# Flamingo block with routed-expert attention: VectorE's gate inversion moved ahead of round 1's row maxima, GpSimd's next mixture begun ahead of the third pair's sums

## The reference

```python
q = (x @ Wq).reshape(b, t, h, dh).transpose(0, 2, 1, 3)
k = (x @ Wk).reshape(b, t, h, dh).transpose(0, 2, 1, 3)
gl_v = (x @ Ws).reshape(b, t, h, e)
wv = _topk_mask(gl_v, SEL) * jax.nn.sigmoid(gl_v)
xv = jnp.einsum('btd,edk->btek', x, Wv)
v = jnp.einsum('bthe,btek->bhtk', wv, xv)
probs = jax.nn.softmax(jnp.einsum('bhid,bhjd->bhij', q * scale, k), axis=-1)
attn = jnp.einsum('bhij,bhjd->bihd', probs, v)
gl_o = (x @ Wd).reshape(b, t, h, e)
out = jnp.einsum('bthe,bthk,ekd->btd', _topk_mask(gl_o, SEL), attn, Wo)
```

## Time and profile before

| | us |
|---|---|
| median of 3 runs | 1139.66 (1139.25 to 1140.4) |
| the profiled execution's own time | 1140.54 |
| its span in the profile | 1138.8 |
| TensorE busy | 1103.0 (97%) |
| VectorE busy | 926.2 (81%) |
| GpSimd busy | 657.9 (58%) |
| ScalarE busy | 568.1 (50%) |

### The profile page before, as it was taken

The page is one execution under the profiler, slowest core; times in us unless marked ns, Lnnn a source line. Parts: engine busy times, 40 slices in busy tenths (PEclk is TensorE's granted clock), DMA queues, the critical chain, the costliest instruction groups (busy, mean ns, idle before and its releaser), DMA issues.

```text
span 1138.8 us, 18705 instructions
## 1 busy us (share of the span) xinstructions
PE 1103.0 (97%) x5709; PEld 836.8 (73%) x5709; DVE 926.2 (81%) x1609; ACT 568.1 (50%) x1295; POOL 657.9 (58%) x476
## 2 busy tenths in 40 slices
PE   7999999999999999999999999999999999999988
PEld 6888888888888888886676766767667666767655
DVE  7988787878777775768798797887988987988986
ACT  7634444444444443436556555455556555555533
POOL 2645252525243433328849669489398497595793
PEclk9999999999999999999999999999999999999999
DMA  5441414141414122343333524424326235244241
GB/s 204 148 139 47 130 56 129 55 129 55 129 55 129 55 92 93 131 130 83 103 76 110 166 55 147 129 55 150 108 59 199 74 94 161 77 116 121 53 134 38
DMA packets 89277, 119.97 MB, mean 105 GB/s; under 512 B 9120, under 2 KB 52896, under 8 KB 89248
## 3 DMA queue, kind: packets, MB, share of 16 engines
q1 hardware_dynamic: 89248, 119.61, 35.1%
HBM read 58.76 MB, written 16.78 MB: 66 GB/s over the span
## 4 chain that ended last, share of the span: by engine, by line
PE 68%; POOL 13%; DVE 9%; issue 5%; ACT 4%; POOLq 0%; DMA 0%; DVEq 0%; ACTq 0%
PE ps_f L992 23%; PE ps_s L992 8%; PE ps_o L2297 7%; PE ps_h L992 7%; POOL spare L1610 6%; PE ps_r L2219 6%; POOL spare L1616 5%; PE ps_r L2252 5%; PE ps_s L2273 4%; PE ps_r L2228 3%; DVE nmax L1880 2%; DVE beaten L1969 1%; POOL z L1628 1%; ACT tmp L1701 1%; ACT probs_odd L1701 1%
## 5 line engine op out<-in xcount | busy, mean ns | idle before, releaser
L1610 POOL TENSOR_TENSOR spare<-xv,pick 128x512 f32<-128x512 f32 x160 | 185.2, 1157 | 35.2 <-DVE pick L1996 22.3
L1880 DVE TENSOR_REDUCE nmax<-ps_s 128x1 f32<-128x512 f32 x256 | 158.6, 681 | 55.0 <-PE ps_s L2273 54.0
L1628 POOL TENSOR_TENSOR z<-z,z_tmp 128x1280 f32<-128x1280 f32 x35 | 102.7, 2934 | 123.5 <-DVE z_tmp L1900 121.0
L1616 POOL TENSOR_TENSOR spare<-spare 128x512 f32<-128x512 f32 x128 | 165.8, 1295 | 10.0
L1701 ACT ACTIVATE tmp<-ps_s,nmax 128x512 f32<-128x512 f32 x124 | 85.5, 689 | 109.5 <-DVE nmax L1880 109.5
L2297 PE MATMUL ps_o<-pt,spare 128*64 128x512 f32 x496 | 115.7, 609 | 9.2 <-POOL spare L1616 5.1
L254 POOL TENSOR_TENSOR e_t<-e_t 128x512 fp32r<-128x512 f32 x28 | 35.4, 1297 | 135.6 <-ACT e_t L510 135.6
L2273 PE MATMUL ps_s<-k,q 64*128 64x512 f32 x768 | 106.3, 408 | 0.7 <-ACT pt L1710 0.7
L2273 PEld LDWEIGHTS ps_s<-k,q 64*128 64x128 f32 x768 | 67.3, 184 | 47.3 <-issue 34.3
L254 POOL TENSOR_TENSOR c<-stage,c 128x512 fp32r<-128x512 f32 x28 | 41.5, 1514 | 95.8 <-ACT c L250 95.8
L2219 PE MATMUL ps_r<-es_t,c_t 128*128 128x512 f32 x384 | 96.3, 399 | 0.0
(11 more groups left out here) (253 smaller groups left out, 2279.1 us busy)
## 6 DMA issues: line engine op xcount, KB each, us to landing
pt<-tmp SPq DMA_DIRECT2D x248, 128.0 KB, 2.6
stage<-in_x SPq DMA_DIRECT2D x32, 256.0 KB, 3.1
x_sb<-in_x SPq DMA_DIRECT2D x8, 1024.0 KB, 5.3
x_dram<-x_sb SPq DMA_DIRECT2D x32, 256.0 KB, 3.2
stage<-x_dram SPq DMA_DIRECT2D x8, 1024.0 KB, 5.5
x_sb<-x_dram SPq DMA_DIRECT2D x8, 1024.0 KB, 5.6
out_dram<-x_sb SPq DMA_DIRECT2D x31, 256.0 KB, 2.7
pt<-probs_odd SPq DMA_DIRECT2D x60, 128.0 KB, 2.7
```

The lines of the kernel that those rows point to most:

```text
L1610: pool.tensor_tensor(v_tmp[:] if e else acc, xv[:, :, e, :].unsqueeze(2).broadcast_to(shape), pick[:, e, :, 2 * p:2 * p + 2].unsqueeze(3). ...
L1616: pool.tensor_tensor(acc, acc, v_tmp[:], ALU.add).then_inc(v_steps, 1)
L1628: pool.tensor_tensor(zv, zv, z_tmp[:, h % 2], ALU.add).then_inc(z_pool, 1)
L1880: dve.tensor_reduce(nmax[:, n:n + 1], ps_s[:, n % BANKS, :], AX_X, ALU.max, negate=True).then_inc(nmax_ready, 1)
```

## The change

VectorE's `invert` and `route_values` of a batch move from round 1, place SCORES, behind the four row maxima, to round 0, place TURNS, right behind `count_values`. On GpSimd `mix_values` takes a range of experts, and the first mixture of batch b+1 is split: experts 0 and 1 (two products and one sum) ahead of the sums of the third pair (heads 4 and 5) of batch b, experts 2 to 4 behind them. The waits for the pick, the expert values and the earlier values product now stand ahead of the first part.

```diff
+        EARLY = 2
...
-            def mix_values(b, p, first=False):
+            def mix_values(b, p, first=False, experts=range(E)):
...
-                if p == 0:
+                if p == 0 and 0 in experts:
                     pool.wait_ge(pick_ready, b + 1)
                     pool.wait_ge(xv_ready, b * NT + NT)
...
-                if not first:
+                if not first and 0 in experts:
 
                     pool.wait_ge(o_ps, b * PAIRS - PAIRS + p + 1)
...
-                for e in range(E):
+                for e in experts:
...
+            def turn_of(b):
+
+                mix_values(b + 1, 0, experts=range(EARLY))
+                mix_sums(b, LAST_PAIR - 1)
+                mix_values(b + 1, 0, experts=range(EARLY, E))
+
             mix_values(0, 0, True)
             rest(0, True)
             with pool.Fori(0, B - 2) as b:
-                mix_sums(b, LAST_PAIR - 1)
-                mix_values(b + 1, 0)
+                turn_of(b)
                 rest(b + 1)
-            mix_sums(B - 2, LAST_PAIR - 1)
-            for p in range(PAIRS):
+            turn_of(B - 2)
+            for p in range(1, PAIRS):
                 mix_values(B - 1, p)
...
                     if 0 <= n < ROUNDS:
                         for tile in range(n * BANKS, n * BANKS + BANKS):
                             row_max(b, tile)
-                    if n == 1:
-                        invert(b)
-                        route_values(b, first)
...
                         compare(b)
                         count_better(b)
                         count_values(b)
+                        invert(b)
+                        route_values(b, first)
```

## The result

| | median us | range, runs | ratio to before |
|---|---|---|---|
| before | 1140.40 | 1139.25 to 1140.92, 7 | |
| changed | 1144.03 | 1142.65 to 1145.17, 7 | 1.0033 [1.0022, 1.0045] |

The change makes the kernel slower by 3.6 us (2.5 to 5.1). The forecast was 1145.5 us (+5.9) with a range from 1142 to 1150 and 0.90 on slower: side and range hold, and the size is over by 2.3 us. The profiled execution took 1142.79 us, its span is 1141.0.

A forecast was written before the change was run, and what follows sets the result against it. The prediction took TensorE's in-order queue as the bound, so only TensorE's waits lengthen a batch. 7 x (1.49 - 0.73) + 0.54 = +5.9 us gave 1145.5 us, with a range from 1142 to 1150.

The forecast's parts named there:

- Insertion: VectorE's moved block ahead of round 1's q difference and row maxima makes these 1.80 us late.
- Loss in round 1: TensorE waits for late exponentials at tile 7's transposes: 1.80 - 0.31 = 1.49 us in each of 7 loop batches.
- The slack: Round 1, tile 7's transposes: they could start at 740.56 but start near 740.87, so 0.31 us is free.
- GpSimd's wait: TensorE's wait for GpSimd's mixture ahead of the first pair's values product goes: 0.73 us a batch.
- Blocking: GpSimd and VectorE sums holding each other up: no change counted, 0.3 us either way per batch for the range.
- the lower end of my range: Insertion of 1.67 and no z wait left (0.24 a batch): +3.1 us, so 1142.8, rounded out to 1142.
- The first batch: Outside the loop: the whole 1.80 us lost, a 1.26 us wait gone, net +0.54 us.
- The 1.26: First batch: TensorE's wait at 559.47, through ScalarE's logits copy held by GpSimd's mixtures, goes: 1.26 us.
- (a): Rival, faster: transposes have more slack, TensorE does not feel late exponentials, only removed waits count: 1133.3 us; chance 0.06.
- (b): Rival, no difference: VectorE and ScalarE catch up, most of the 1.0 us expert projections wait goes: 1139.3 us; chance 0.04.
- (c): Rival: GpSimd's shifted instructions block VectorE's two sums by a whole instruction each: 1157 us, half gives 1151; chance 0.05.
- (d): Rival: a pause makes the granted clock fall, a values product takes 6.12 us instead of 3.65: 1163 us; chance 0.02.

The follow-up runs named there:

- experiment 1: Kernel before with VectorE's half alone (reciprocal, pick and mask moved; GpSimd's order as before): 1143.64 us, ratio 1.0034.
- the doses: Kernels with insertions of 0, 0.28, 1.13 and 1.80 us, which lost 0.02, 0.11, 0.98 and 1.62 us in the part with round 1.
- experiment 3: Kernel before with GpSimd's half alone, but one early product ahead of the third pair's sums instead of two: 1135.04 us, ratio 0.9956.
- experiment 4: Kernel before with the reciprocal alone moved ahead of the q difference and the maxima: 1141.88 us, ratio 1.0015.
- experiments 6 and 7: First: kernel before, last batch's turned-block moves issued ahead of the residual load, 1139.00 us. Second: that together with experiment 3, 1131.52 us.

## Why the prediction was right, and where its size was off

**Insertion, 1.80 forecast.** 1.80 in the change and in experiment 1.

**Loss in round 1, 1.49 forecast, 1.62 measured.** ScalarE's last read, relative to the batch's start, is 1.83 later (742.49 + 0.21 = 742.70, against 740.51, less the 0.36 by which this batch started later):

```profile
742.49 0.21 ACT L1707 ACTIVATION_READ_ACCUMULATOR spare<-ps_s,nmax 128x1 f32 x1
```

Tile 7's transposes start 0.05 behind it, as forecast. The slack was mis-sized. Half of the eight's 0.96 gave 740.87 for tile 7's start before; TensorE's timeline of before has it at 740.82:

```profile
740.82 0.60 PE L2281 MATMUL ps_s<-ident,spare 128*128 128x128 f32 x4
```

So the slack was 0.26 and not 0.31, and with the read 1.83 late 1.57 is lost at that point. The other 0.05 is a term that I had not seen: tile 7's four transposes take 0.58 to the start of the values product when a wait releases them (742.75 to 743.33), and took 0.53 in the row of eight (740.82 to 741.35). The usable slack is therefore about 0.2, which the doses confirm. The three terms (0.03, 0.05 and 0.05) add 7 x 0.13 = 0.9 us to the sum.

**GpSimd's wait, -0.73.** It is gone, but I gave the credit to the wrong edit. My own numbers could have told: the old mixture would have ended near 762.0 (761.89 + 0.13), and TensorE arrives at 762.65 in any case. Experiment 1 shows it gone with GpSimd untouched. The sum is the same either way; the verdict on the two halves isn't.

**Blocking, "I count no change".** This is the step that failed most. The second part of the batch is 1.07 shorter, and the 0.73 is not all of it. TensorE's timeline of before, to be laid beside the rows from 759.90 on above:

```profile
757.95 0.60 PE L2281 MATMUL ps_s<-ident,spare 128*128 128x128 f32 x4
758.72 0.66 PE L2281 MATMUL ps_s<-ident,spare 128*128 128x128 f32 x4 [0.18 <-ACT spare L1701]
759.62 1.53 PE L2242 MATMUL ps_r<-ident,z 128*128 128x128 f32 x12 [0.25 <-DVE z L1911]
```

From the z transposes to the values product it was 2.27 (759.62 to 761.89) and is 1.46, as in experiments 1 and 3: the mixture's wait was worth 0.81, 0.08 more than its listed 0.73. Up to the z transposes it was 18.27 from the fourth pair's product (741.35 to 759.62) and is 18.01 (743.33 to 761.34): the other **0.26**. Most of it lies between round 3's transposes and those of z, 1.67 before (757.95 to 759.62) and 1.44 now. The eight alone take 0.96, so the waits in this place have shrunk and not gone. They hang on VectorE's two sums of z: the first stands ahead of round 3's row maxima, the second ahead of the z transposes. These took 1.72 and 2.07 in that batch before. In the changed kernel:

```profile
753.71 1.62 DVE L1917 TENSOR_TENSOR z<-z,z_tmp 128x1280 f32<-128x1280 f32 x1
...
759.38 1.90 DVE L1917 TENSOR_TENSOR z<-z,z_tmp 128x1280 f32<-128x1280 f32 x1
```

GpSimd's instructions beside them:

```profile
752.67 1.31 POOL L1617 TENSOR_TENSOR spare<-spare 128x512 f32<-128x512 f32 x1
...
757.75 2.18 POOL L1611 TENSOR_TENSOR spare<-xv,pick 128x512 f32<-128x512 f32 x2 [0.16 <-POOL spare L1617]
```

The first sum starts 0.27 ahead of the end of a GpSimd instruction (753.98), the second 0.55 ahead (759.93). Over the 1.44 of an undisturbed one they take 0.18 and 0.46 more: what was left of the other's instruction, less 0.09. Before, they took 0.91 more together, now 0.64: 0.27 less, which is TensorE's 0.26.

GpSimd's half is not what did it, as experiment 1 shows, with GpSimd's order untouched. Its two sums, in VectorE's timeline:

```profile
754.21 1.48 DVE L1911 TENSOR_TENSOR z<-z,z_tmp 128x1280 f32<-128x1280 f32 x1
...
759.74 2.08 DVE L1911 TENSOR_TENSOR z<-z,z_tmp 128x1280 f32<-128x1280 f32 x1
```

And its z sums in GpSimd's timeline:

```profile
743.65 5.92 POOL L1628 TENSOR_TENSOR z<-z,z_tmp 128x1280 f32<-128x1280 f32 x2 [15.46 <-DVE z_tmp L1900]
```

VectorE's two take 0.68 more together than two undisturbed ones, and TensorE reaches the z transposes 18.05 after the fourth pair's product (743.83 to 761.88), so 0.22 of the 0.26 is there already. GpSimd's z sums follow VectorE's product for head 4, which the insertion makes only 0.15 late, while TensorE, and the VectorE work that waits for it, is 1.6 late. So in both kernels GpSimd's z sums start 0.18 ahead of the fourth pair's product (743.15 against 743.33, in experiment 1 743.65 against 743.83), where they started 1.29 behind it (742.64 against 741.35), and all of GpSimd's work behind them meets VectorE's sums in another phase. I had looked for new phases in GpSimd's half alone. That the new phase came out as a gain was luck: nothing in the prediction could tell its sign. In experiment 3, with one early product and no insertion, it is 18.25, the old value.

The Trainium skill ("SBUF — State Buffer", the section on SBUF's two separate sides) says that whichever starts first keeps the other out until its end. These rows agree but for the 0.09, and add that the price lies between nothing and a whole instruction, by phase. The two early products, beside VectorE's row maxima with their input from PSUM, took 2.18 against 2.19, as my reading of that rule had it. That the sum of the blocking stays as it is was not in the rule, and did not hold.

The total is 7 x -0.26 = -1.8 us; the lower end of my range had 0.24 a batch for it. The 0.08 that the mixture's wait was worth beyond its listed time makes -0.6 more.

**The first batch, +0.54 forecast, -0.28 measured.** From GpSimd's clearing of its buffer to the next batch's first scores it took 78.98 and takes 78.70. The 1.26 is gone, and the loss is there, 1.68 up to that place. TensorE's timeline, where eight transposes ran in 1.25 before:

```profile
514.01 0.66 PE L2286 MATMUL ps_s<-ident,spare 128*128 128x128 f32 x4 [0.78 <-ACT spare L1707]
515.35 0.66 PE L2286 MATMUL ps_s<-ident,spare 128*128 128x128 f32 x4 [0.68 <-ACT spare L1707]
```

A wait of 0.39 for an exponential at 540.25 of before went too, which I had not counted. The last 0.3 I can't give to one row.

**The sum.** 7 x (1.62 - 0.81 - 0.26) - 0.28 = +3.6 (forecast +5.9), and by the measured batches 7 x 0.53 - 0.28 = +3.4; the medians differ by 3.6. The 2.3 by which I was over is what three errors leave: +0.9 in round 1, -2.4 in the rest of the batches, -0.8 in the first batch. The profiled execution grew by only 2.25, since the last batch's values product behind the long pause took 5.35 in place of 6.12 (its first four us show a clock of 0.57 instead of 0.50) and the first half was 0.4 shorter. TensorE's timeline:

```profile
1110.01 5.35 PE L2302 MATMUL ps_o<-pt,spare 128*64 128x512 f32 x16 [4.16 <-issue]
```

**The rivals.** (a) fell: the exponentials bind. By the doses it would have decided at an insertion of about 0.18 + 0.81 = 0.99 (forecast 1.04); that of experiment 4, 1.13, lies over it and costs 0.20 a batch. (b) fell: the 1.0 for the expert projections stayed at 1.0. (c) fell, and with the other sign. (d) did not occur: with pauses of 0.53 and 0.68 a batch the clock stayed at 1.00.

## What to carry to other kernels

In this kernel an instruction moved ahead of a row of work that the bounding engine is fed from cost what it inserted less the slack there, whatever it brought forward. Read that slack first, as the distance from the producer's end to the consumer's start. And look at a change's two halves apart: here the VectorE half cost all that the change cost, and removed GpSimd's wait only by being late, the GpSimd half alone took three instructions into a gap that held one, and the same idea with one product, and nothing moved on VectorE, gained 4.6 us.

## What was unexpected in the hardware's behaviour

- Blocking between VectorE and GpSimd depends on the phase to a tenth of a microsecond. The same 128 x 1280 sum took 1.48 to 2.09 us within the kernel of experiment 1. There the insertion on VectorE alone, by shifting the engines against each other, brought TensorE to the z transposes 0.22 us a batch sooner without making any work less.
- Tile 7's four transposes take 0.58 us to the next row's start when a wait releases them, and 0.53 in a row of eight. The wait for the mixture, listed with 0.73, was worth 0.81.
- A pause of about 4 us ahead of the last batch's values product left the clock at its lower level of 1.2 GHz for most of the product: 5.35 and 6.12 us in two executions, and more in experiment 3, by TensorE's timeline:

```profile
1101.09 6.52 PE L2303 MATMUL ps_o<-pt,spare 128*64 128x512 f32 x16 [4.30 <-issue]
```

  Behind pauses of 1.30 and 2.13 in experiments 6 and 7 it took 3.65. Where the pause was made that short, both it and the product behind it took less.
